# The border rows of a blur: sixteen multiply-adds on the vector engine in place of matrix products

## What is computed

```python
x = x + _L0_conv_ref(_gn(x), ...)      # Haar transform, 1x1 conv, norm, gelu, 3x3 depthwise,
                                       # norm, 1x1, gelu, 1x1, residual, 1x1, norm, gelu, inverse Haar
x = x + _L1_conv_ref(_gn(x), kernel)   # kernel: 4x4 blur, [1,3,3,1] x [1,3,3,1] / 16

def _L1_conv_ref(input, kernel):       # PAD0, PAD1 = 2, 1
    k = jnp.flip(kernel, (0, 1))
    xp = jnp.pad(input, ((0, 0), (0, 0), (PAD0, PAD1), (PAD0, PAD1)))
    return lax.conv_general_dilated(xp, k per channel, (1, 1), 'VALID', feature_group_count=c)
```

## Time and profile before

| | |
|---|---|
| median of 3 runs | 5608.24 us (5605.93 to 5615.25) |
| the profiled execution | 5612.93 us, its span 5611.1 us, granted clock 0.976 |
| PE busy | 5223.0 us, 93% |
| DVE busy | 4318.1 us, 77% |
| ACT busy | 3702.3 us, 66% |
| POOL busy | 2095.5 us, 37% |
| DMA | 1729.80 MB, mean 308 GB/s |

### The profile page before, as it was taken

How to read it: one execution, slowest core, us unless ns; L and a number is a source line. 1 busy time by engine, 2 the same in 40 slices (tenths; PEclk the granted TensorE clock), 3 DMA queues, 4 the chain that set the end, 5 groups by cost and what they waited for, 6 DMA issues and landing times. The chain is left out here.

```text
span 5611.1 us, 67501 instructions
## 1 busy us (share of the span) xinstructions
PE 5223.0 (93%) x18280; PEld 3171.0 (57%) x18280; DVE 4318.1 (77%) x5293; ACT 3702.3 (66%) x4976; POOL 2095.5 (37%) x1393
## 2 busy tenths in 40 slices
PE   2888888899999999997699999999999999999999
PEld 1333333334555555563266666666666667667777
DVE  8555555418999999966988888888888888888833
ACT  0333333346777777756788788787887878878754
POOL 0000000017777777742333333333333333333354
PEclk9999999999999999999899999999999999999999
DMA  9999999942333333326999999999999999999986
GB/s 372 367 383 387 376 382 377 354 147 81 106 107 108 106 109 107 105 87 258 382 388 403 394 404 399 394 404 390 395 399 388 404 392 395 404 382 404 394 273 221
DMA packets 829589, 1729.80 MB, mean 308 GB/s; under 512 B 50064, under 2 KB 587152, under 8 KB 718608
## 3 DMA queue, kind: packets, MB, share of 16 engines
q1 hardware_dynamic: 485136, 1121.34, 53.8%
q10 hardware_dynamic: 344064, 604.05, 28.1%
HBM read 1050.95 MB, written 674.23 MB: 307 GB/s over the span
## 5 line engine op out<-in xcount | busy, mean ns | idle before, releaser
L1159 POOL TENSOR_TENSOR y_lo<-y_centred_tile,y_hi 128x1024 fp32r<-128x1024 f32 x512 | 1039.7, 2052 | 1721.1 <-ACT y_centred_tile L1509 1405.3
L1380 PE MATMUL blur_psum<-y_hi,band_hi 128*128 128x512 f32 x4096 | 1128.9, 417 | 8.8 <-DVE y_tile L1248 7.4
L1380 PE MATMUL blur_psum<-y_lo,band_hi 128*128 128x512 f32 x4096 | 1042.5, 396 | 7.5 <-POOL y_lo L1159 7.1
L1363 PE MATMUL conv_psum<-u_in,w_conv 128*128 128x512 f32 x2048 | 958.1, 610 | 84.2 <-DMA u_in<-u_scratch 36.1
L1380 PEld LDWEIGHTS blur_psum<-y_hi,band_hi 128*128 128x128 f32 x4096 | 765.8, 188 | 278.9 <-issue 100.6
L1380 PEld LDWEIGHTS blur_psum<-y_lo,band_hi 128*128 128x128 f32 x4096 | 769.7, 188 | 200.8 <-POOL y_lo L1159 16.5
L1220 DVE TENSOR_TENSOR pair_sums<-gelu_out,conv_psum 128x512 f32<-128x512 f32 x960 | 613.9, 683 | 308.3 <-ACT conv_psum L1471 308.0
L1248 DVE SCALAR_TENSOR_TENSOR y_tile<-blur_psum,rstd_all,y_tile 128x1024 f32<-128x1024 f32 x512 | 639.5, 1276 | 159.7 <-PE blur_psum L1380 152.2
L1471 ACT ACTIVATE gelu_out<-conv_psum,bn_shift,bn_scale 128x512 f32<-128x512 f32 x512 | 397.9, 777 | 522.0 <-PE conv_psum L1363 498.9
L1363 PEld LDWEIGHTS conv_psum<-u_in,w_conv 128*128 128x128 f32 x2048 | 393.8, 195 | 525.3 <-issue 384.2
L396 PE MATMUL z_psum<-x_resident,w_folded 128*128 128x512 f32 x1280 | 600.0, 624 | 28.0 <-ACT z_psum L425 19.1
(11 more groups left out here) (175 smaller groups left out, 5661.9 us busy)
## 6 DMA issues: line engine op xcount, KB each, us to landing
x_tile<-x SPq DMA_DIRECT2D x256, 1024.0 KB, 9.1
y_scratch<-x_tile ACTq DMA_DIRECT2D x256, 1024.0 KB, 7.7
y_tile<-y_scratch SPq DMA_DIRECT2D x512, 512.0 KB, 12.5
out<-y_tile ACTq DMA_DIRECT2D x512, 512.0 KB, 9.7
x_stream<-x SPq DMA_DIRECT2D x192, 1024.0 KB, 11.6
x_resident<-x SPq DMA_DIRECT2D x160, 1024.0 KB, 11.2
z_scratch<-z_tile ACTq DMA_DIRECT2D x256, 256.0 KB, 7.2
z_in<-z_scratch SPq DMA_DIRECT2D x256, 256.0 KB, 3.0
```

The source lines that it names most:

```text
L1159: nc.gpsimd.tensor_tensor(y_lo[:, h, part, 2:2 + W], y_c[:, part, :], y_hi[:, h, part, 2:2 + W].bitcast(F32), ALU.subtract).then_inc(s_lo, 1)
L1363: nc.tensor.matmul(cv[s][:], w[:, s * C:(s + 1) * C], u_t[:, k % US, :], start=True, stop=True).then_inc(s_mm, 1)
L1380: ins = nc.tensor.matmul(bl[t][:, 2 * c:2 * c + 2, :], wt[:, kw, :], y[:, h, ch:ch + 2, kw:kw + W], start=(m == 0 and kw == 0), stop=(m == ...
```

## The change

The strip isn't multiplied by PE any more. SP loads it four times, one copy for each tap row kh, each shifted by a row, so that 48 partitions (sixteen channels by three rows) hold what each output row needs; the columns are cut in two halves, the left one on partitions 0 to 47 and the right one on 64 to 111. That is eight transfers of 48 rows of 130 or 129 columns in place of two, and two stores of 48 rows of 128 columns in place of one. ACT takes off the mean in place, in two activations. DVE sums sixteen tap products in `seam_sum`, four at the end of each unit (`seam_quarter`), each waiting for the one before, then scales and adds, then takes the mean's part back, into `seam_out`, of which there are two in place of four. The products, the split into hi and lo, POOL's part, the bands of the strip, and PE's waits for the strip's bank are gone. The waits for buffers are changed to fit.

```diff
+LAG_QUARTER = LAG_SPLIT + 2
+LINKS_SEAM = 17
@@ SP
-                    sp.wait_ge(s_sc, b * NQ - NQ + q + 1)
-                    sp.dma_start(seam_t[:, q % 2, :], yr[bass.ds(n * GRP, 16), 125:131, :]).then_inc(s_sin[q % 2], 16)
-                    sp.wait_ge(s_sst[q % KS], b * (16 * NQ // KS) - 16 * NQ // KS + 16 * (q // KS) + 16)
-                    sp.dma_start(keep_t[:, q % KS, :], yr[bass.ds(n * GRP, 16), 127:130, :]).then_inc(s_sin[q % 2], 16)
+                    sp.wait_ge(s_sdn, b * NQ - NQ + q + 1)
+                    for half, (to, cols) in enumerate(SEAM_PARTS):
+                        for kh in range(4):
+                            sp.dma_start(seam_t[64 * half:64 * half + 48, q % 2, kh, to],
+                                         yr[bass.ds(n * GRP, 16), 125 + kh:128 + kh, cols]).then_inc(s_sin[q % 2], 16)
@@ POOL
-                    nc.gpsimd.tensor_tensor(seam_lo[:, 2:2 + W], seam_c[:],
-                                            seam_hi[:, 2:2 + W].bitcast(F32), ALU.subtract).then_inc(s_slo, 1)
@@ DVE
+            def seam_quarter(b, phase, k):
+                qq, j = divmod(k - LAG_QUARTER, QUAD)
+                at = b * NQ - NQ + qq
+                links = b * (NQ * LINKS_SEAM) + (qq - NQ) * LINKS_SEAM
+                y = seam_t[:, qq % 2]
+                if j == 0:
+                    dve.wait_ge(s_sc, 2 * at + 2)
+                for kw in range(4):
+                    tap = KR[0:SEAM_P, 4 * j + kw:4 * j + kw + 1]
+                    window = y[:, j, kw:kw + SEAM_W]
+                    done = 4 * j + kw
+                    if done or phase != SECOND or qq > 0:
+                        dve.wait_ge(s_slk, links + done)
+                    if done == 0:
+                        ins = nc.vector.tensor_scalar(seam_acc[:], window, tap, None, ALU.mult)
+                    else:
+                        ins = nc.vector.scalar_tensor_tensor(seam_acc[:], window, tap, seam_acc[:], ALU.mult, ALU.add)
+                    ins.then_inc(s_slk, 1)
+                if j < 3:
+                    return
+                ...
+                nc.vector.scalar_tensor_tensor(seam_o[:, slot, :], seam_acc[:], rs_s[:, bass.ds(at, 1)],
+                                               y[:, 2, 2:2 + SEAM_W], ALU.mult, ALU.add).then_inc(s_slk, 1)
+                dve.wait_ge(s_slk, links + 17)
+                nc.vector.tensor_scalar(seam_o[:, slot, :], seam_o[:, slot, :], nm_s[:, bass.ds(at, 1)], None,
+                                        ALU.subtract).then_inc(s_sdn, 1)
@@ DVE, end of a unit
-                        if (k - LAG_BLUR) % QUAD == QUAD - 1:
-                            take_seam(b, k)
                         take(b, k, 0)
                         take(b, k, 1)
+                    if group_at(b, phase, k, LAG_QUARTER) is not None:
+                        seam_quarter(b, phase, k)
@@ PE
-                        if blurring and (k - LAG_BLUR) % QUAD == QUAD - 1:
-                            seam(b, phase, k, seam_products)
@@ ACT
+                for half, (inside, _) in enumerate(SEAM_PARTS):
+                    part = seam_t[64 * half:64 * half + 48, q % 2, :, inside]
+                    nc.scalar.activation(part, part, ACT.Identity,
+                                         bias=nm_s[64 * half:64 * half + 48, bass.ds(at, 1)]).then_inc(s_sc, 1)
```

More of the change, by code:

```diff
@@ L748, in band_column @@
                 for kh in range(4):
[L749 to L757 removed]
+                    mask = K[:, K_TM + kh * 128:K_TM + (kh + 1) * 128]
+                    scalar = KR[:, kh * 4 + kw:kh * 4 + kw + 1]
+                    if kh == 0:
+                        lk.link(nc.vector.tensor_scalar(band[:, kw, :], mask, scalar, None, ALU.mult))
+                    else:
+                        lk.link(nc.vector.scalar_tensor_tensor(band[:, kw, :], mask, scalar, band[:, kw, :],
+                                                               ALU.mult, ALU.add))
             def band_parts():
                 lk.link(nc.vector.tensor_copy(band_hi[:], band))
[L761 removed]
                 lk.link(nc.vector.tensor_tensor(band_lo[:], band, band_hi[:].bitcast(F32), ALU.subtract))
[L763 removed]
             dve.wait_ge(s_w, 48)
@@ L941 @@
 YS = 8
-KS = 4
+KS = 2
+SEAM_P = 112
+SEAM_W = W // 2
 AHEAD3 = 2
@@ L1055, in phase_tail @@
         block = ctx.enter_context(nc.Block())
+        SEAM_PARTS = ((slice(2, SEAM_W + 3), slice(0, SEAM_W + 1)), (slice(0, SEAM_W + 2), slice(SEAM_W - 2, W)))
         def quad_views(k):
@@ L1142, in _ @@
             pool.memset(quarter[:], 1.0 / GRP).then_inc(s_set, 1)
-            for y in (seam_hi, seam_lo):
-                for cols in (slice(0, 2), slice(2 + W, PADW)):
-                    pool.memset(y[:, cols].bitcast(F32), 0.0).then_inc(s_set, 1)
+            pool.memset(seam_t[:], 0.0).then_inc(s_sdn, 2)
             pool.wait_ge(s_v, 5)
@@ L1272, in body @@
                     return
-                for k in range(LAG_BLUR if phase == END else UNITS):
+                for k in range(LAG_QUARTER if phase == END else UNITS):
                     if phase <= MIDDLE:
@@ L1384, in blur @@
                 ins.then_inc(s_t, 1)
-            def seam(b, phase, k, products):
-                q = (k - LAG_BLUR) // QUAD
-                at = b * NQ - NQ + q
-                pe.wait_ge(s_shi, at + 1)
-                pe.wait_ge(s_slo, at + 1)
-                if phase <= MIDDLE:
-                    pe.wait_ge(s_ge, b * (4 * UNITS) + 4 * k + 3 + 4)
-                elif k == LAG_BLUR - 1 and phase == DRAIN:
-                    pe.wait_ge(s_tab, b)
-                if k != LAG_BLUR + QUAD - 1 or phase != SECOND:
-                    pe.wait_ge(s_sev, at)
-                for m, (wt, y) in enumerate(products):
-                    for kw in range(4):
-                        ins = nc.tensor.matmul(small[0:48, 0:W], wt[:, kw, :], y[:, kw:kw + W],
-                                               start=(m == 0 and kw == 0),
-                                               stop=(m == len(products) - 1 and kw == 3))
-                ins.then_inc(s_smm, 1)
             def gn2_average(b, phase):
```

108 lines of the change are left out of this document (35 added, 73 removed).

## The result

| | before | after |
|---|---|---|
| median | 5607.53 us | 6295.32 us (6290.79 to 6299.81) |
| ratio | | 1.1223, 95% interval 1.1209 to 1.1236 |
| profiled span | 5611.1 us | 6298.0 us |

What follows compares the result with a forecast made beforehand. PE was taken to bound the kernel before; a DVE-POOL cycle then adds 54.75 quads by 13.8 = 756 us, plus 11 for drain and end, to 5611.1: 6378 span, median 6375 us. Range 5990 to 6500.

Steps and rivals of the forecast that it cites:

- PE bounds before: Main loop before: PE sets the pace, quad (four units) 44.6 us, the strip's eight products costing 1.03 us of it.
- rival 2: Main loop: multiply-adds hide in DVE's idle time and the gain arrives, 5552 us, or no change; chance 0.06.
- Without exclusion: Main loop, DVE and POOL not excluding each other: DVE becomes the bound at 44.8 us a quad, nothing gained.
- Rival 3: Main loop: DVE is the bound without exclusion, 44.8 to 45.5 us a quad, 5620 to 5670 us; chance 0.08.
- The closed cycle: Main loop: residual, square, y_hi, y_c, POOL, quad sum, POOL, quad sum, residual; quad 58.4 us, 13.8 more.
- That POOL gets in between the two quad sums: DVE's unit: waiting POOL runs when the first quad sum ends, ahead of the second; forecast 6375 us, chance 0.48.
- rival 1: DVE's quad sums run as one block, POOL cannot get between: quad 53.2 us, 6090 us; chance 0.29.
- What stops ACT: ACT's square needs the residual, starting 0.43 us after its end R; POOL follows 6.12 us later, at R+6.55.
- Past R+8.7: Leaving the cycle needs POOL after the second quad sum, past 8.7 us from residual's end, over 2 us later.
- The sum: Whole kernel: 54.75 quads by 13.8 is 756, plus 11 for drain and end: 6378 us span, 6375 median.
- DMA and SP edits at nothing: SP's eight small strip loads, two stores and new wait cost nothing; ten issues fit inside a 58 us quad.
- Rival 4: Main loop: PE's clock falls to 1.2 GHz, or SP's wait reaches loads and PE: 6465 to 6900 us; chance 0.09.

Runs made afterwards that it cites:

- the last experiment: Changed kernel without multiply-adds, all eight strip loads, only the left half of each x tile loaded after the first batch: 5569.17 us, ratio 0.9927.
- part 1: Changed kernel with POOL's two subtractions cut to 4 columns: 5610.12 us; or replaced by one 128x4 subtraction and two memsets: 5611.21 us.
- the one-input sums: Changed kernel with each of the sixteen multiply-adds replaced by a one-input sum along the same operand: 5843.29 us, ratio 1.0400.
- the gate and the move: Changed kernel, POOL's subtractions also waiting for the unit's residual, multiply-adds moved behind the pair sums one unit later: 5629.07 us, ratio 1.0037.
- the move alone: Changed kernel with the multiply-adds moved behind the pair sums, without the new POOL wait: 5859.07 us, ratio 1.0444.
- part 4: Kernel before without seven of eight strip products: 5591.40 us; changed kernel without multiply-adds, with two of eight strip loads: 5578.40; with half x loads: 5569.17.

## Why the prediction was right, point by point

**PE bounds before:** right, and not the whole of it. DMA share 1.05 stood in the earlier trace rows and was passed over. The strip's 1.03 us a quad on PE is near (0.95: 43.65 for 44.6 in the last experiment), but rival 2's 56 us could not have arrived: of 49 us that PE alone was spared, 17 did.

**A multiply-add of 0.386 with its gap:** right. Four in a row take 1.50 us (1.54 forecast), ACT's two new activations 1.47 (1.5).

**Without exclusion a quad of 44.8:** 44.53 measured, twice (part 1): in undisturbed quads DVE's own bound is 0.2% from where PE's was. Rival 3's 5620 to 5670 fits: with the drain as it was those kernels would have come to about 5625.

**The closed cycle:** right in its order, its holds and its size. POOL between the quad sums and again ahead of the residual; a plain unit of 14.53 forecast, 14.40 measured; a quad of 58.4 and 58.3. In the last quarter's unit POOL is first, as worked out, and from residual's end to residual's end the four units are 14.34, 14.40 twice and 15.17, where 14.46, 14.53 twice and 14.89 were forecast; the last is the longer because POOL asks at R+6.82 there. That DVE's lateness alone keeps the cycle closed is shown by the one-input sums, that the order is the loss by the gate and the move. Of PE's share the prediction said near 75%; it is 84%, with the same work at a lower clock.

**That POOL gets in between the two quad sums** was the choice between the forecast (0.48) and rival 1 (0.29), and in part luck: it rested on DVE having got in between POOL's two. With the multiply-adds behind the pair sums (the move alone) the same assumption gave 6150 to 6300 and 5859 was measured.

**What stops ACT:** right. ACT's square waits 241.3 us for residuals after. It starts 0.7 us behind one's end (4299.08, 4299.80) and not 0.43, so POOL asks at R+6.85 and not R+6.55, and DVE's quad sums start at R+6.24 and not R+6.36. POOL is 0.61 us late in them where 0.19 was worked out; since its turn comes at the end of the first one either way, the unit doesn't change by it. DVE leaves the cycle if POOL comes much later, which the gate with the move shows. "Past R+8.7" was too strict for a partial escape: in the change itself single units are 12.60 where POOL asks at about R+7.6, in the second quad sum, and holds up the residual alone.

**The sum:** forecast 6378 of span, measured 6298.0, and the 80 us are nearly all in one term. From the 37th residual to the last one 219 units take 2485.95 us before and 3167.40 after: +681.5, where 54.75 x 13.8 gave 756. A batch before is 365.3 us, 8 x 44.6 and 8.5 more for the long units at its start. I left these "as they are", that is, added to the new cycle too. After, a batch is 461 to 467 us, which is 8 x 58.3 (466) and nothing more. That the waits of those units lie inside DVE's cycle, where it waits anyway, is my reading; no run separates it. 6.8 batches by 8.5 are 58 of the 75; units of 12.6 where POOL came late make up most of the rest. The drain and the end were put at +11 and are +2 (299.66 us behind the last residual, then 301.62).

**DMA and SP edits at nothing:** right for the kernel after (an issue of the strip's eight loads has a median of 0.563 us, the DMA share is 0.88), because the cycle slows the transfers with the rest. Out of the cycle it is wrong, by 35 us for six of the eight loads (part 4). The gated version has undisturbed quads of 44.05 against 44.6 and is still 21 us above the kernel before; its y_hi waits 213 us for y_tile. That the loads are its loss is argued from that, not shown; that DVE's 6.8 us leave it no slack is another candidate.

**Rivals.** Rival 1 is refuted for this order of work (4.16 us for two quad sums), and its order happens in the moved one (2.35, then 3.97). The Trainium skill's page SBUF — State Buffer, section Who interferes with whom, has issue order decide who waits; for a DVE that issues two in a row, these two runs show both outcomes. Rival 4's clock: the granted clock fell to 0.92 in the stretch, and PE had cover (301.62 busy us of 360).

## What to carry to other kernels

Before giving a nearly full engine more work, ask what it excludes, and lay out the instants at which the other engine asks: here 6.8 us of work in a quad cost 13.7, because two engines that had missed each other began to meet, and each meeting brought on the next. Such an order can be set by hand: a wait that sends the other engine's reads under instructions that don't mind them, and a move that takes one's own new work out of their way, gave back 666 of 687 us, where either alone gave back 336 and 436. And a DMA share at 1 can be a bound in waiting: relieving the engine in front of it pays only as far as the transfers let it.

## What the runs showed of the hardware

A POOL memset of 128x1024 (0.95 us) and a DVE instruction with two SBUF inputs run together at full speed, while a POOL subtraction of four columns waits 2.3 us for the same instruction. POOL, waiting, is let in between two DVE instructions that follow each other without a wait (quad sums 4.16 us) or only behind both (2.35), with asks at 0.61 and 0.86 us into the first against 0.72: behind pair sums it got in between in 286 of 302 meetings, the other 16 being those where it asked at 1.13 us or later; behind multiply-adds in none of 75. And one program can hold two rhythms for most of a batch, about 365 and 451 to 455 us, and in the one trace of it the change came in a batch's first units.
